# Five groups' source rows picked column by column from the transposed x in SBUF, in a graph attention layer

## What is computed

```
Q, K, V = x @ Wq + bq, x @ Wk + bk, x @ Wv + bv      # 6250 x 8 heads x 12
E = edge_attr @ We + be                              # 100000 x 8 x 12
score = exp(clip(sum_d(K[src] * Q[dst] / sqrt(12) * E), -5, 5))
h = segment_sum(V[src] * score, dst) / (segment_sum(score, dst) + 1e-6)
out = layernorm(x + h)                               # all float32
```

## Time and profile before

| | |
|---|---|
| median of three runs | 1008.33 us (1006.75 to 1008.42) |
| the profiled execution: span from first to last instruction | 1007.7 us |
| the page gives no other time of that execution; the median less the span | 0.6 us |
| mean granted TensorE clock | 0.877 of full speed |
| instructions in the trace | 13429 |

### The profile page before, as it was taken

One profiled execution on the slowest core, in us unless ns is written; L12 is line 12 of the kernel. 1 busy time (PEld: TensorE's weight loads), 2 busy tenths in 40 slices (PEclk: granted clock), 3 DMA queues, 4 the chain that ended last, 5 costly groups with the idle time before them and its releaser, 6 DMA issues.

```text
span 1007.7 us, 13429 instructions
## 1 busy us (share of the span) xinstructions
PE 753.4 (75%) x3375; PEld 414.5 (41%) x3375; DVE 595.0 (59%) x1583; ACT 452.3 (45%) x1094; POOL 745.0 (74%) x790
## 2 busy tenths in 40 slices
PE   5999977777778777777777766877767877777763
PEld 4756633333344333433444333443334444343332
DVE  4459955555555655565556566565565656565664
ACT  3477733444444444444444444444444444444431
POOL 6677777777777777777777777777777777777772
PEclk9899998989888898889897998779989878989885
DMA  9987765555555555546555555555555555555321
GB/s 226 323 225 190 210 172 150 153 158 151 149 151 142 140 151 140 141 129 160 139 142 140 149 142 138 150 136 144 149 137 157 139 146 146 142 141 156 99 78 47
DMA packets 124522, 153.26 MB, mean 152 GB/s; under 512 B 57885, under 2 KB 92191, under 8 KB 124436
## 3 DMA queue, kind: packets, MB, share of 16 engines
q0 software_dynamic: 37008, 75.28, 29.1%
q1 hardware_dynamic: 80608, 73.74, 25.9%
q10 hardware_dynamic: 6822, 3.31, 1.3%
HBM read 142.26 MB, written 9.98 MB: 151 GB/s over the span
## 4 chain that ended last, share of the span: by engine, by line
POOL 52%; issue 29%; DMA 11%; DVE 4%; SPq 1%; PE 1%; ACT 0%; POOLq 0%; DVEq 0%
POOL kv L499 52%; DMA kv<-kv_table,src_idx 9%; DMA q_table<-node_stage 1%; DMA w_all<-biases_in 1%; DVE node_stage L747 1%; DVE ps_last L772 1%; DVE node_stage L786 1%; SPq L410 0%; DVE stats L834 0%; SPq L409 0%; DVE kq L765 0%; PE ps_eq L979 0%; ACT node_stage L560 0%; DVE node_stage L830 0%; DVE node_stage L822 0%
## 5 line engine op out<-in xcount | busy, mean ns | idle before, releaser
L499 POOL DMA_INDIRECT kv<-kv_table,src_idx x750 | 712.1, 949 | 232.2 <-issue 220.3
L606 ACT ACTIVATE ps_last<-clipped 128x32 f32<-128x32 f32 x196 | 39.4, 201 | 496.5 <-DVE clipped L779 496.5
L1035 PE MATMUL ps_eq<-pick_t,q_win 128*96 128x512 f32 (+1 forms) x262 | 157.9, 689 | 19.1 <-ACT e_t L601 17.7
L765 DVE TENSOR_TENSOR kq<-kv,ps_eq_qe 128x384 f32<-128x384 f32 x98 | 54.1, 552 | 189.0 <-DMA kv<-kv_table,src_idx 186.4
L1028 PE MATMUL ps_eq<-ea,w_all 128*96 128x512 f32 (+1 forms) x262 | 156.5, 683 | 7.2 <-DVE qe_t L755 5.7
L765 DVE TENSOR_TENSOR kq<-kv,ps_qe_seg 128x384 f32<-128x384 f32 x98 | 54.0, 551 | 174.4 <-DMA kv<-kv_table,src_idx 174.1
L1060 PE MATMUL ps_last<-node_stage 128*104 128x80 f32 x780 | 103.5, 283 | 60.9 <-DVE acc_t L801 51.1
L1060 PE MATMUL ps_qe_seg<-node_stage 128*104 128x80 f32 x784 | 101.6, 279 | 59.8 <-DVE acc_t L801 48.1
L592 ACT ACTIVATE distance<-rel_bc,neg_part 80x512 bf16<-80x512 bf16 x196 | 138.4, 706 | 2.0 <-issue 1.1
L595 ACT ACTIVATE pick_t<-distance 80x512 f32<-80x512 bf16 x196 | 123.2, 629 | 6.2
L1060 PEld LDWEIGHTS ps_last<-node_stage 128*104 128x104 f32 x780 | 92.5, 196 | 70.2 <-DVE node_stage L786 59.1
(11 more groups left out here) (89 smaller groups left out, 656.4 us busy)
## 6 DMA issues: line engine op xcount, KB each, us to landing
ea<-ea_t_in SPq DMA_DIRECT2D x196, 192.0 KB, 2.8
rel_bc<-rel_rows_dram SPq DMA_DIRECT2D x196, 80.0 KB, 2.8
kv<-kv_table,src_idx POOLq DMA_INDIRECT x750
q_win<-q_table SPq DMA_DIRECT2D x196, 30.0 KB
kv_table<-node_stage SPq DMA_DIRECT2D x5, 576.0 KB, 5.9
x_both<-x_t_in SPq DMA_DIRECT2D x5, 480.0 KB, 13.6
x_both<-x_rows_in ACTq DMA_DIRECT2D x10, 240.0 KB, 3.4
out<-node_stage SPq DMA_DIRECT2D x11, 192.0 KB, 3.2
```

The source lines that it names most:

```text
L499: pool.indirect_dma_start(rows[0:n, :], None, table, bass.IndirectOffsetOnAxis(ap=src_idx[0:n, tile:tile + 1], axis=0)).then_inc(semaphore ...
L765: nc.vector.tensor_tensor(kq[:, group % 2, 0:n, :], kv[:, slot, 0:n, 0:DIM], ps_qe[group % 2][:, 0:n * DIM].rearrange("p (t d) -> p t d", ...
L1035: nc.tensor.matmul(ps_eq[(2 * group + 1) % 3][0:DIM, 0:n], q_win[:, slot, :], pick_t[:, group % 3, 0:n], start=True, stop=True).then_inc(e ...
```

## The change

The rows of K and V of five whole groups (`LOCAL`: 56, 88, 120, 152, 184) are no longer gathered. Their source numbers are loaded into SBUF as `src_row`. In 32 iterations for each of the five, from group 8 to group 167, ACT and DVE each load eight node numbers into registers and copy eight columns of `x_t` (97 partitions, one element in each) into `early_t`. In eight later iterations TensorE multiplies 128 of the picked columns by the K or the V weights, one product for each iteration, next to the output of `turn` in its PSUM bank, and DVE copies the result (128 x 96) to the group's slot in `kv`, ten to seventeen groups ahead of its use. GpSimd skips these groups.

Because `x_t` must stay, `x_n` is gone: SP loads x by nodes in thirteen steps into `y`, the buffer of the results, and reloads a slot when its store has ended.

```diff
+COLS_ACT, COLS_DVE = 8, 8
+LOCALS, LOCAL_FIRST, LOCAL_SETTLE, LOCAL_LEAD = 5, 8, 6, 10
+LOCAL_ROUNDS = GROUP // (COLS_ACT + COLS_DVE)
+PRODUCTS_AT = [LOCAL_FIRST + (i + 1) * LOCAL_ROUNDS + LOCAL_SETTLE for i in range(LOCALS)]
+LOCAL = [at + LOCAL_LEAD for at in PRODUCTS_AT]
...
+        def columns_of(engine, local, first, n):
+            return nc.values_load_multi_w_load_instructions(
+                src_row[local:local + 1, first:first + n], engines=[engine], min_val=0, max_val=N_NODES - 1,
+                skip_runtime_bounds_check_because=NODES)[1]
...
             def windowed(streamed):                                  # GpSimd
                 for group in range(EARLY, GROUPS):
+                    if group in LOCAL:
+                        continue
...
+            def copy_columns(group):                                 # ACT; DVE's is the same with tensor_copy
+                local, round_ = local_round(group)
+                if local is None:
+                    return
+                if local >= 2 and round_ == 0:
+                    act.wait_ge(n_kv, 2 * GROUP_TILES * (local - 1))
+                first = round_ * COLS_ACT
+                for i, node in enumerate(columns_of(mybir.EngineType.Activation, local, first, COLS_ACT)):
+                    last = nc.scalar.copy(early_t[:, local % 2, first + i:first + i + 1], x_t[:, bass.ds(node, 1)])
+                last.then_inc(c_cols_act, 1)
...
                     if group < GROUPS:                               # ACT's loop
                         exponentials(group)
-                    part, between = divmod(group - X_PARTS_FROM, X_PARTS_EVERY)
-                    if 0 <= part < X_PARTS and between == 0:
-                        load_x_by_node(part)
+                    copy_columns(group)
...
             def times_keys(group):                                   # DVE
-                for t in range(n):
-                    dve.wait_ge(*landed(group * GROUP_TILES + t))
+                if group in LOCAL:
+                    dve.wait_ge(n_kv, 2 * GROUP_TILES * (LOCAL.index(group) + 1))
+                else:
+                    for t in range(n):
+                        dve.wait_ge(*landed(gathered_before(group) + t))
...
+                for local, t, half in product_at(group):
+                    at = LOCAL[local] % KV_RING
+                    if t == half == 0:
+                        dve.wait_ge(e_msg, LOCAL[local] - KV_RING + 1)
+                    nc.vector.tensor_copy(kv[:, at, t, half * DIM:(half + 1) * DIM], local_of(group)).then_inc(n_kv, 1)
...
                     if group >= ADDED:                               # DVE's loop
                         accumulate(group - ADDED)
+                    copy_columns(group)
...
+            def local_product(group, local, t, half):                # TensorE, from turn(group)
+                if t == half == 0:
+                    pe.wait_ge(c_cols_act, LOCAL_ROUNDS * (local + 1))
+                    pe.wait_ge(c_cols_dve, LOCAL_ROUNDS * (local + 1))
+                return nc.tensor.matmul(local_of(group), early_t[:, local % 2, t * P:(t + 1) * P],
+                                        w_all[0:DIM + 1, half * DIM:(half + 1) * DIM], start=True, stop=True)
...
+            def load_x(step):                                        # SP
+                slot, first, n = step % FINAL_RING, FIRST_TILES[step], tiles_in(step)
+                if step >= FINAL_RING:
+                    sp.wait_ge(f_out[slot], 16 * stores_before(step))
+                sp.dma_start(y[:, slot, 0:n, :], x_rows.rearrange("(t p) d -> p t d", p=P)[:, first:first + n, :]
+                             ).then_inc(l_xn[slot], 16)
...
-                nc.vector.tensor_tensor(h[:, s, 0:n, :], h[:, s, 0:n, :], x_n[:, first:first + n, :], ALU.add
+                nc.vector.tensor_tensor(h[:, s, 0:n, :], h[:, s, 0:n, :], y[:, s, 0:n, :], ALU.add
```

More of the change, by code:

```diff
@@ L83 @@
 GENERAL, WINDOWED, STREAMED = 0, 1, 2
+COLS_ACT, COLS_DVE = 8, 8
[3 more added lines that the diff above has]
+LOCAL = [at + LOCAL_LEAD for at in PRODUCTS_AT]
+NODES = "sources are node numbers below N_NODES"
 IN_RANGE = "the least of node numbers below N_NODES, and of N_NODES where edges are padded"
@@ L96, in tiles_of, with gathered_before, local_round, product_at @@
     return min(GROUP_TILES, TILES - group * GROUP_TILES)
+def gathered_before(group):
+    return GROUP_TILES * (group - sum(g < group for g in LOCAL))
+def local_round(group):
+    local, round_ = divmod(group - LOCAL_FIRST, LOCAL_ROUNDS)
+    return (local, round_) if 0 <= local < LOCALS else (None, None)
+def product_at(group):
+    return [(i, *divmod(group - at, 2)) for i, at in enumerate(PRODUCTS_AT) if 0 <= group - at < 2 * GROUP_TILES]
 def edges_in(tile):
@@ L273, in build @@
         l_dst = sem("l_dst")
-        l_xn = sem("l_xn")
+        l_xn = [sem(f"l_xn{i}") for i in range(FINAL_RING)]
+        l_src_row = sem("l_src_row")
+        c_cols_act = sem("c_cols_act")
+        c_cols_dve = sem("c_cols_dve")
+        n_kv = sem("n_kv")
         c_xones = sem("c_xones")
@@ L344, in landing_of, with landed @@
         def landing_of(group, t):
-            return e_kv[(group * GROUP_TILES + t) % IN_FLIGHT]
-        def landed(tile):
-            return e_kv[tile % IN_FLIGHT], 16 * (tile // IN_FLIGHT + 1)
+            return e_kv[(gathered_before(group) + t) % IN_FLIGHT]
+        def landed(gathered):
+            return e_kv[gathered % IN_FLIGHT], 16 * (gathered // IN_FLIGHT + 1)
         def node_sums(step, streamed):
@@ L355, in node_sums, with local_of @@
             return bank[:, WINDOW:WINDOW + FINAL_TILES * SUMS]
+        def local_of(group):
+            return ps_qe[group % 2][:, GROUP_TILES * DIM:][:, 0:DIM]
         early_cols = EARLY * GROUP_TILES
@@ L463, in windowed @@
                         load_window(group, base)
+                    while quad >= 2 and loaded < min(stored + FINAL_RING, STEPS):
+                        load_x(loaded)
+                        loaded += 1
                     while (streamed and stored < STREAMED_STEPS
@@ L470, in windowed @@
                     store_result(step)
+                    if step + FINAL_RING in range(loaded, STEPS):
+                        load_x(step + FINAL_RING)
                 all_stored()
             def general():
+                all_tables_stored(sp)
+                for step in range(FINAL_RING):
+                    load_x(step)
                 for slot in range(EA_RING):
@@ L481, in general @@
                     store_result(step)
+                    if step + FINAL_RING < STEPS:
+                        load_x(step + FINAL_RING)
                 all_stored()
@@ L872, in finish_nodes, with copy_columns @@
                 normalise_last()
+            def copy_columns(group):
+                local, round_ = local_round(group)
+                if local is None:
+                    return
+                if local >= 2 and round_ == 0:
+                    dve.wait_ge(n_kv, 2 * GROUP_TILES * (local - 1))
+                first = LOCAL_ROUNDS * COLS_ACT + round_ * COLS_DVE
+                for i, node in enumerate(columns_of(mybir.EngineType.DVE, local, first, COLS_DVE)):
+                    last = nc.vector.tensor_copy(early_t[:, local % 2, first + i:first + i + 1],
+                                                 x_t[:, bass.ds(node, 1)])
+                last.then_inc(c_cols_dve, 1)
             def windowed(streamed):
                 all_tables_stored(dve)
+                dve.wait_ge(x_mm, 2 * EARLY)
+                dve.wait_ge(l_src_row, 16)
                 for group in range(GROUPS + 1 if streamed else GROUPS + ADDED):
@@ L1047, in turn @@
                                                qe_t[:, group % QE_RING, t * P:(t + 1) * P], ident[0:DIM, 0:DIM])
+                for local, t, half in product_at(group):
+                    last = local_product(group, local, t, half)
                 last.then_inc(e_turn, 1)
```

40 lines of the change are left out of this document (17 added, 23 removed).

## The result

The changed kernel takes 981.75 us (median of four runs, 980.7 to 982.24) against 1008.25 of the kernel before (1006.75 to 1008.42): a ratio of 0.974, with a 95% interval from 0.9727 to 0.9753, so 26.5 us less. The forecast was 983.2. The profiled execution spans 980.3 us (before 1007.7) at a granted TensorE clock of 0.907.

A forecast was written before the change was run, and what follows sets the result against it. GpSimd's descriptor work for gathers was taken to pace the kernel. Skipping 20 gathers at 1.2545 us takes 25.1 us off 1008.3, everything added costing nothing: 983.2 us, range 981 to 1000 with about 0.83 of the chance.

The forecast's parts named there:

- What paces: Main loop: GpSimd's descriptor work for gathers paces everything from 49.85 to 989.44 us, at 1.2545 us a gather.
- The size: Gathers on POOL: five groups of four skipped, 20 x 1.2545 = 25.1 us saved, none of it hidden.
- DVE's loop: DVE, groups 8 to 167: loads and column copies add 1.5 us to 2.78, 4.3 an iteration, bounds 3.8 to 5.1.
- ACT's copy: Column copies on ACT: 0.15 us each, 1.6 us an iteration with the load, against 2.54 idle; upper bound 3.6.
- third rival: Loop on DVE or ACT becomes the bound, above T = 4.85 us; upper bounds end at 1023 or 1183 us; chance 0.11.
- The shared port: DVE's 1280 SBUF copies against POOL's gathers: no loss taken; bounds nothing, and 69 us if whole rows hold gathers.
- first two rivals: Gathers held by DVE's column copies: by single copies, 9 us, end 992, chance 0.14; by whole rows, 69 us, 1052, chance 0.06.
- The rest at nothing: Products on PE, their copies on DVE, SP's loads of x, the src_row load and DVE's entry waits cost nothing; tail unchanged.

The follow-up runs named there:

- the first experiment: Changed kernel with all added copies and products, but GpSimd gathers all 196 groups again, against the kernel before: 1008.70 us, ratio 0.9983.

## Why the prediction was right

- **What paces** was right. With all of the added work but all gathers the time is 0.9983 of before, with the 20 gathers skipped and none of the loads and column copies 0.9735, with both 0.974. The gain is the gathers, to within the 2 us that these intervals leave.
- **The size** was 25.1 us and came out at 26.5 by the medians. The missing 1.4 is for the most part the closer spacing of the other gathers, 729 steps of 1.2523 against 1.2545 us. I had kept the spacing. Only 0.2 us of the difference is the late gathers (four before, three after, late by 1.07 and 0.84 us in all); the rest is some 2 ns a gather, and the traces do not tie it to the change: without the columns the spacing is 1.2548, with everything gathered 1.2533, and on one and the same chip 1.2555 with seven groups and 1.2517 with eight. So the forecast's 25.1 was the right term, and that it came within 1.4 us is as near as such scatter allows (729 steps of 4 ns are 2.8 us).
- **DVE's loop** was estimated at 4.3 us, between 3.8 and 5.1; where it waits for nothing it is mostly 3.82 or 4.21. The copy was put at 0.13 and is 0.115 apart, the load at 0.5 and is 0.60 with 0.2 to 0.5 of it uncovered. DVE's remaining wait was to be 95 us and is 119.7, ACT's was to be 220 and is 280.7: both of the costs were a little too high (on DVE 1.3 us a round by the waits, where 1.5 was taken).
- **ACT's copy** was put at 0.15; it is (0.84 - 0.187)/7 = 0.093, below the nearest row. The bound of 0.36 from four wide activations was far off, and so was the 1183 us built on it. The load of eight is 0.55 us there.
- **The loop as the bound** (third rival) is a real mechanism: sixteen columns on DVE, at 5.75 us an iteration, go over the 4.85 and take 1106.6 us; eight groups, whose iterations mostly take 4.53 to 4.94 us where DVE waits for nothing, stay under it, and POOL waits there for DVE in no piece over 0.3 us. The point itself lies between the two; no run comes nearer.
- **The shared port** (first two rivals): no loss, as taken, but the reason that was weighed, one element or more, is only half of it. By the rule of the Trainium skill's "Advanced Engine Details and Errata", section "2x-2p Requirements", one element does not take the second port; the runs agree (153 to 156 ns for one element, up to 425 for two). But pairs cost the kernel nothing either. What decided is when a copy starts and how long it is: a gather is held only by an instruction that started more than 0.04 us before it and still runs 0.13 us after its start, so by none shorter than 0.17, and a column copy lasts 0.154. The prediction's two bounds, 9 us for single copies held on average for half their length and 69 for a whole row as one block, assumed that any copy across the sensitive point holds the gather. The late gathers of the earlier trace rows both have an instruction that started 0.12 and 0.14 us before them; that was there to be read. By the Trainium skill's "SBUF — State Buffer", section "SBUF: two separate sides", of a two-port VectorE instruction and a GpSimd one whichever starts first gets the shared pair for its whole instruction and the other blocks. The runs agree where VectorE starts first (46 of 46 long copies). Where the gather starts first they show less than that: a copy that starts 0.06 to 0.49 us behind it is not stretched.
- **The rest at nothing** (SP's loads, products, tail): shown together, with the new place of x, by the first experiment. The products are copied ten to three groups ahead of their use, not ten to seventeen. The stretch behind the last kq is 980.3 - 966.2 = 14.1 us, before 14.6.

What I had not thought of is that another chip may be paced by something else.

## What to carry to other kernels

Find the engine that has no free time, count what is taken off it, and then ask only whether the others have room: here 1.3 us in a loop of 5.0 with 2.2 free. Compute how long the loop of each other engine may get: that one number (4.85 us) told beforehand that the change was safe at 4.3, that sixteen columns on DVE were not at 5.5, and that eight groups, at 4.7, would be close; that they fit was left to the run. Before taking a loss from contention, look which of the two instructions in the rows started first. A gain that lives on another engine's free time holds only where that time is free, so try it on more than one chip.

## What the runs showed of the hardware

- Register loads from SBUF by count of numbers: 4 in 0.34 us on DVE and 0.30 on SP; 8 in 0.60 on DVE and 0.55 on ACT; 12 in 0.85 on DVE; 16 in 1.02 on ACT. That is about 0.06 us a number and 0.09 to start with.
- Copies of one column at a run-time address follow each other in 0.115 us on DVE and 0.093 on ACT, the address calculation included.
- A gather of 0.95 us contends with DVE at two places. At its start, whichever starts first wins: an fp32 copy within SBUF (97 x 384) or an addition of two SBUF inputs that started more than 0.04 us earlier and still runs 0.13 us after the gather's start holds it to its own end (46 and 42 cases), and a two-element copy or an addition that starts from 0.04 us before to 0.03 after it is itself delayed, by up to 0.075. From about 0.51 to 0.78 us after the gather's start, copies within SBUF of two elements or more that start there are stretched, by up to 0.26 us; additions are not (558 ns wherever they start there), and one-element copies never are.
- Two of the four chips on which the experiments ran took a third longer for the kernel before (1339.29 and 1320.52 us). The changed kernel and its variants show there 17 to 41 stretches of over 2 us in which PE, DVE and ACT all idle, and 167 to 431 address calculations of over 0.15 us, most of them 0.7, instead of 0.046 (DVE) and 0.037 (ACT).
